# The token table read out of PSUM before the shared expert's third sum, and the last group's lanes shared out anew

## The reference

```python
# layer 0: attention pooling, then a mixture of experts
attn_in = tanh(einsum('bsd,da->bsa', hidden, W1) + b1)
scores  = einsum('bsa,a->bs', attn_in, v)
p       = softmax(where(mask, scores[:, None, :], -1e30))      # one of three masks for each sequence
pooled  = einsum('bjl,bld->bjd', p, hidden) / cnt[..., None]

w, idx = gate(xf, wg)                    # 4 of 32 experts for each token, with group limits
pos  = (cumsum(one_hot(idx)) * one_hot(idx)).sum(-1) - 1
dest = where(pos < cap, expert * cap + pos, E * cap)            # cap = 640 slots for each expert
buf_tok[dest] = tok                      # which token sits at each of the 32 * 640 slots
xe  = xp[buf_tok].reshape(E, cap, DIM)
h   = silu(xe @ w1) * (xe @ w3)
out = h @ w2 * buf_w
z   = silu(xf @ sw1) * (xf @ sw3) @ sw2  # the shared expert, over all tokens
# layer 1: a matrix chosen for each sequence, layernorm, attention with rotary embedding,
# layernorm, a second mixture of 8 experts (2 for each token, gelu)
```

## Time and profile before

| | before |
|---|---|
| median of three runs | 1525.67 us |
| the profiled execution: its time | 1527.01 us |
| the profiled execution: its span | 1525.2 us |
| PE busy | 1392.3 us, 91% of the span |
| PE weight loads busy | 1221.8 us, 80% |
| DVE busy | 1033.8 us, 68% |
| ACT busy | 906.0 us, 59% |
| POOL busy | 721.4 us, 47% |

### The profile page before, as it was taken

One profiled execution on the slowest core, in us unless ns is written; L12 is line 12 of the kernel. 1 busy time (PEld: TensorE's weight loads), 2 busy tenths in 40 slices (PEclk: granted clock), 3 DMA queues, 4 the chain that ended last, 5 costly groups with the idle time before them and its releaser, 6 DMA issues.

```text
span 1525.2 us, 27526 instructions
## 1 busy us (share of the span) xinstructions
PE 1392.3 (91%) x9776; PEld 1221.8 (80%) x9776; DVE 1033.8 (68%) x2435; ACT 906.0 (59%) x2156; POOL 721.4 (47%) x720
## 2 busy tenths in 40 slices
PE   7997699999999999589999999999519999999996
PEld 5876599999999998358778777777419999998996
DVE  2999477777777775567888988895526556556552
ACT  5886255555555543158888888888526546456452
POOL 0788653444344204435465665653252435445333
PEclk9998899999999999689999999999859999999999
DMA  5421256566666614287868678686351343234212
GB/s 171 146 78 37 62 161 181 170 186 180 177 178 186 181 53 123 53 138 139 170 119 165 151 142 172 130 134 104 111 141 21 90 104 95 58 79 100 39 22 28
DMA packets 139449, 182.00 MB, mean 119 GB/s; under 512 B 22486, under 2 KB 107297, under 8 KB 139313
## 3 DMA queue, kind: packets, MB, share of 16 engines
q1 hardware_dynamic: 111152, 128.28, 33.6%
q0 software_dynamic: 28160, 51.96, 16.8%
HBM read 107.28 MB, written 42.08 MB: 98 GB/s over the span
## 4 chain that ended last, share of the span: by engine, by line
PE 78%; DVE 9%; issue 5%; POOL 3%; DMA 2%; ACT 2%; SPq 1%; POOLq 0%; DVEq 0%; ACTq 0%
PE banks L921 50%; PE banks L1365 5%; PE banks L1322 5%; PE banks L1412 3%; PE banks L440 3%; PE banks L983 2%; PE banks L1378 2%; PE banks L1339 2%; DVE lane_at L504 1%; PE banks L1759 1%; PE banks L1426 1%; DVE X L1561 1%; POOL table L1314 1%; PE banks L1346 1%; PE banks L1337 1%
## 5 line engine op out<-in xcount | busy, mean ns | idle before, releaser
L921 PE MATMUL banks<-hi_x,hi_w 128*128 128x320 f32 (+1 forms) x832 | 286.8, 345 | 10.7 <-DVE hidden L956 5.1
L921 PE MATMUL banks<-lo_x,hi_w 128*128 128x320 f32 (+1 forms) x832 | 285.6, 343 | 0.0
L921 PE MATMUL banks<-hi_x,lo_w 128*128 128x320 f32 (+1 forms) x832 | 285.2, 343 | 0.0
L921 PE MATMUL banks<-hi_w,hi_h 128*128 128x256 f32 x896 | 260.2, 290 | 2.1 <-DVE X L1010 1.7
L921 PE MATMUL banks<-lo_w,hi_h 128*128 128x256 f32 x896 | 253.5, 283 | 0.0
L921 PE MATMUL banks<-hi_w,lo_h 128*128 128x256 f32 x896 | 253.5, 283 | 0.0
L863 POOL DMA_INDIRECT xe<-pooled,idx x160 | 156.3, 977 | 198.6 <-PE banks L983 149.2
L1746 POOL DMA_INDIRECT out<-X,tab x64 | 106.5, 1664 | 204.7 <-DVE X L1843 190.1
L1459 ACT ACTIVATE PN<-banks,smax 128x256 f32<-128x256 f32 (+1 forms) x512 | 180.3, 443 | 15.9 <-DVE smax L1553 15.9
L921 PEld LDWEIGHTS banks<-hi_x,hi_w 128*128 128x128 f32 x832 | 158.3, 190 | 24.3 <-issue 10.4
L921 PEld LDWEIGHTS banks<-hi_w,hi_h 128*128 128x128 f32 x896 | 171.2, 191 | 3.3 <-issue 1.3
(11 more groups left out here) (186 smaller groups left out, 3051.4 us busy)
## 6 DMA issues: line engine op xcount, KB each, us to landing
w<-in_L_ffn_w SPq DMA_DIRECT2D x96, 256.0 KB, 5.8
done<-res SPq DMA_DIRECT2D x32, 640.0 KB, 3.9
QS<-parts_qk SPq DMA_DIRECT2D x128, 128.0 KB
KS<-parts_qk SPq DMA_DIRECT2D x128, 128.0 KB, 8.1
BIG<-in_L_ffn_W SPq DMA_DIRECT2D x16, 1024.0 KB, 9.6
mask<-in_c_masks SPq DMA_DIRECT2D x16, 257.0 KB, 2.8
pooled<-XF SPq DMA_DIRECT2D x16, 256.0 KB, 3.2
WS<-in_L_cond_W SPq DMA_DIRECT2D x16, 256.0 KB, 5.7
```

What stands on the lines that cost most here:

```text
L921: last = e.matmul(o, a[i], b[j], start=start and k == 0, stop=stop and k == 2, skip_group_check=True)
```

## The change

The read of the table is moved. `dve_found` is called in DVE's list directly before the `split_h` of the shared expert's third part, item 1 (`lo_h` (2, 1)), instead of after the loop. Its three instructions and their waits are the same.

The sharing of lanes and steps is changed for the last group alone (columns 28 to 31): DVE makes three of the four lanes (two before), POOL one (two before), and ACT all four steps (three before), so POOL none. For the other groups it stays as it was.

```diff
-    KD, KA = 2, 3
-
-    def lanes_at(e, g, q, ks, done):
+    def lane_shares(g):
+
+        return (3, 4) if g == NGR - 1 else (2, 3)
+
+    def lanes_at(e, g, q, ks):
         n = R * g + q
         e.wait_ge(s_parts, g + 1)
         if n >= 2:
...
-        if done:
-            last.then_inc(done, 1)
+        return last
 
     def pool_lanes(e, g, q):
         n = R * g + q
-        lanes_at(e, g, q, range(KD, K0), None)
-        for k in range(KA, K0):
+        kd, ka = lane_shares(g)
+        last = lanes_at(e, g, q, range(kd, K0))
+        for k in range(ka, K0):
             last = e.tensor_scalar(step_at[:, n % 2, k, :], stairs, parts_f[:, g % 2, 0, q, k:k + 1], 2.0, ALU.is_lt, ALU.mult)
         last.then_inc(s_lane, 1)
...
-        for k in range(KA):
+        for k in range(lane_shares(g)[1]):
             last = e.activation(step_at[:, n % 2, k, :], stairs, ACT.Sign, bias=parts_f[:, g % 2, 0, q, k:k + 1], scale=-1.0)
...
-                lanes_at(e, g, *d, range(KD), s_dve_lane)
+                lanes_at(e, g, *d, range(lane_shares(g)[0])).then_inc(s_dve_lane, 1)
...
             elif step == "split_h":
+                if (g, *d) == (NSH - 1, 1):
+                    dve_found(e)
                 dve_split_h(e, g, *d)
...
-        dve_found(e)
```

## The result

The changed kernel took 1516.98 us, the median of four runs (1516.01 to 1518.1), against 1526.26 us for the kernel before on the same chip: a ratio of 0.9938, with a 95% interval of 0.9922 to 0.9953. Forecast were 1518.3 us and 7.4 us less; measured were 9.3 us less. In a later comparison the same kernel gave 1518.52 against 1526.57, 8.05 us less (0.9953, interval 0.9936 to 0.9969).

What follows compares the result with a forecast made beforehand. The expert stage was taken as bound by PE, its start delayed by the late bank 7 read on DVE. 7.17 + 0.3 - 0.3 + 0.2 = 7.4 us off 1525.67 gave 1518.3 us, range 1514.9 to 1521.9.

Steps and rivals of the forecast that it cites:

- the read no longer stands behind three X additions: DVE's read of bank 7, moved behind X (1, 0), starts at about 165.9 instead of 173.07: 7.17 us gained.
- the lanes: last `find` without POOL's wait: Last group's lanes and steps: PE's last `find` no longer waits for POOL; 0.3 us more, bounds 0 and 0.5.
- the gathers: neighbours on DVE and landing: First expert's five gathers on POOL: 0.3 us lost beside DVE instructions, 0.2 won in landing.
- the turn of the first expert: first transposes to first up product: PE's turn before the first products: 4.2 us as before if the clock falls, thought likelier; 3.3 if not.
- the products at half clock: First expert's products on PE: 2.9 us at half clock as before; 1.7 if the clock holds.
- sum at the second expert: All terms up to the expert stage, which keeps the gain: 7.4 us less; chance 0.72.
- The landing of the fifth: Data of the fifth gather: 2.96 us may go to 2.7 as weights move later; 0.2 won, bounds -0.3 to +0.3.
- Rival A: PE's clock holds through the shorter hole before the first transposes: 2.1 us more, 1516.2 us; chance 0.18.
- Rival B: Expert stage bound by weights or splits catches up: 1525.7 us, milder form 1522 to 1523; chance 0.08.
- Rival C: DVE's last-group lanes are slow, 1.42 us each: 1532 us, deciding from 0.9 us a lane; chance 0.02.

Runs made afterwards that it cites:

- the third repetition: Both edits, the changed kernel's code a third time, against the kernel before: 1518.52 us against 1526.57, ratio 0.9953.
- both, second time: Both edits, the changed kernel's code once more, against the kernel before on a chip with pauses: 1648.01 us against 1657.43, ratio 0.9955.
- the ten unread matmuls' second run: Both edits plus ten matmuls with unread results before the first transposes, repeated on a chip with pauses, against the kernel before: 1666.16 us against 1677.87, 0.9939.
- the ten matmuls: Both edits plus ten matmuls with unread results before the first transposes, against the kernel before: first 1516.76 us against 1526.57, 0.994; repeated on another chip, 0.9939.

## Why the prediction was right, point by point

All from the `find` of column 28, in us:

| step of the prediction | forecast | measured |
|---|---|---|
| the read no longer stands behind three X additions | 7.17 | 7.16 (move only against before) |
| the lanes: last `find` without POOL's wait | 0.3 | 0.58 on top of the move (0.25 alone) |
| the gathers: neighbours on DVE and landing | -0.1 | 0.27 (from read to transposes, 9.72 to 9.45) |
| the turn of the first expert: first transposes to first up product | 0 | 0.46 (4.20 to 3.74) |
| the products at half clock | 0 | -0.4 (21.68 to 22.09 from first up to the second expert's run of 66) |
| sum at the second expert | 7.4 | 8.06 (49.68 to 41.62), 8.05 in the third repetition |

The mechanism was as told: what bound the start of the experts was the place of the read in DVE's list, and 7.16 of the 8.06 us come from there. The expert stage is bound by PE, so the gain stays: in the third repetition the median moved by 8.05 us.

The terms that were mis-sized most are the turn, by 0.46, and the gathers, by 0.37, 0.8 us together; the products at half clock, put at 0, took 0.4 of that back. The prediction said -0.1 for the gathers, with 0.3 us lost to `lo_w` beside the fifth. In the profile after that gather takes 0.95 us, as alone: it ended (170.76 + 0.95) when `lo_w` had run for 0.2 us. The sixth, beside which `lo_w` runs in full, took 1.02, in the kernel with the move only 1.28; neither is waited for. The landing of the fifth went from 2.96 to 2.68, as forecast in size; it is 2.66 with the move only, but 2.81 with the lanes only, where the gathers did not move (181.84 - 178.99, less the 0.04 to the transposes), so about half of that difference is what two executions differ by, and its cause, the later weight transfers, is not shown. The Trainium skill, in "SBUF — State Buffer", section "Who interferes with whom", says that a DVE instruction with two SBUF inputs contends with a GpSimd instruction that reads SBUF. The 1.23 against 1.39 of the first gather agrees in sign, in one profile, and is 0.16 us, not the 0.44 that I had read into that row.

For the turn I had only two cases, a clock that falls (4.2 us, as before) and one that holds (3.3). I also had misread when it fell before: the earlier trace rows have 0.64 in the stretch from 176 to 177, which is a fall at about 176.3, 3.9 us after the last matmul and not 4.2; no term of the sum uses it. In the profile after it fell, which was the likelier case in the prediction, but at about 174.3, in the middle of the transposes; so the first of them still ran at full clock (8 in 1.28 us instead of 1.97) and the turn took 3.74. The clock then came back 3.9 us after the first up product, where it had been 2.9, and took 0.4 back. That both comparisons give 8.06 and 8.05 is in part luck: in both profiles the clock fell 16.5 to 16.6 us after the `find` of column 28. In the profile "both, second time" it fell at 18.3, behind the transposes, and came back 5.8 us after the first up product. The turn then took 3.48 us, and by the estimate of 0.4 us for each us at half clock the gain would be about 0.5 us smaller, near the 7.4 of the sum. There is one profile of the kernel before, so how far its own 49.68 varies is open.

The lanes gave 0.58 where 0.3 was forecast within bounds of 0 and 0.5, so they passed the upper bound by 0.08. The `find` of column 30 no longer stood behind POOL's step either (before, that step ended at 162.75 and the `find` started at 162.80), so everything behind it, X (1, 0) included, was sooner, by 0.25 us. The prediction saw that X (1, 0), and no longer the last `find`, would set the start of the read, but left X (1, 0) where it was and had an earlier `find` before only in its upper bound. In the profile of both edits the read starts 0.60 us after X (1, 0), without a wait; with the move only, it waits 0.23 us for the last `find`. Another small miss: with the lanes changed, `down` (1, 1) no longer begins right behind the last `find` but waits 0.37 us for X (1, 0), off the path.

In the first comparison the two profiles differ by 8.9 us: 8.06, and 1.3 of luck in the stretch before the last group, less 0.5 that is gone by the end of the span. The medians of four runs differ by 9.3, with an interval of 7.2 to 11.9, which holds the 8.06. No step of the prediction could have had the rest.

Rival A (the clock holds) did not come about by itself, but its price, 2.1 us, was measured as 2.0 when the clock was held by unread matmuls. The parts of this sum agree less well: the turn gave 0.26 us (3.74 to 3.48) where 0.9 was forecast, and the products 1.75 (22.09 to 20.34) where 1.2 was, because after the change less of the turn and more of the products had been at half clock. Rival B (the expert stage catches up) is refuted: of the 9.36 us by which the profile after is ahead at the second expert, 8.9 are left at the end of the span. Rival C (slow lanes) is refuted: six lanes of DVE took 1.83 us, 0.30 each, where 0.9 was its point of decision.

## What to carry to other kernels

When a stage ends with a result that the next stage waits for, look at what stands in front of the instruction that reads it in its engine's list: here three additions, each tied to matmuls that had nothing to do with the table, cost 7.2 us. Measure such a change from the last instant that it leaves as it was, since the stretch before varied by 3.5 us between executions of code that is the same up to there. And a gain in front of a PE at half clock can be given back in part (1.0 of 1.27 us in the one profile here), because the clock need not return sooner with it: count it only behind the point at which the clock is full, or keep PE busy through the hole in front (worth 2.0 us here, in one profile).

## What was not expected of the hardware

On three chips the kernel before took 1657 to 1678 us instead of 1526. In the profiles there, engines stop for 5 to 15 us, and what the profile names as the reason is only "issue" (nothing that it shows) or "remote" (another core or an unknown queue). This is the table of waits between 182 and 196 us of the ten unread matmuls' second run (total, times, longest):

```profile
DVE hidden L959 <- issue: 11.9, 1, 11.9
ACT gate L950 <- remote: 11.8, 1, 11.8
PEld banks L924 <- DVE hidden L959: 8.9, 1, 8.9
```

DVE and ACT stop together right behind the first up products, in the kernel with the lanes only as in those with the move, while the profiles before and after and those on the chip of the third repetition have no such wait there (3.7 us is the longest that either waits there without a named engine). What they wait for is not shown. Ratios on these chips are uncertain by 0.2 to 0.35%, while the stretch up to the first up product agreed between chips within 0.3 us (19.35 to 19.59 for both edits, 19.29 and 19.59 with the ten matmuls).

A second point is the unread matmuls: with four of them between the last transposes and the first product, that product started 2.17 and 2.64 us behind these transposes instead of 1.4 to 1.7, though each takes 0.22 us and PE idled 0.98 us there in the profile after. Two profiles, on chips with pauses, show it.
